# The 64-expert stage: eleven buffers for the blocks' activations, down products ten blocks behind, gates in groups of four tiles, and the first eleven blocks on ScalarE and GpSimd

## What is computed

```python
x = layernorm(hidden).reshape(-1, 128)             # T = 2048 tokens
shared = silu(x @ sg_w.T) * (x @ su_w.T) @ sd_w.T  # one expert of width 128 for all tokens
scores = sigmoid(x @ gate_w.T) + gate_bias         # T x 64
group_scores = scores.reshape(T, 8, 8).max(-1)     # keep the best 4 groups of 8 experts
masked = scores * mask_of_best_groups
topk_w, topk_i = top_k(masked, 6); topk_w /= topk_w.sum(-1) + 1e-8
comb = zeros(T, 64).at[topk_i].add(topk_w)         # the gates: 6 of 64 are not zero
h = silu(x @ eg_w[e].T) * (x @ eu_w[e].T)          # every expert e, width 64, every token
out = hidden + shared + sum_e comb[:, e] * (h @ ed_w[e].T)
```

## Time and profile before

| what | us |
|---|---|
| median of 3 runs | 1375.47 (1373.68 to 1376.39) |
| the profiled execution | 1376.14 |
| its span, from the first to the last instruction | 1374.3 |
| PE busy in the span | 1128.8 |
| DVE busy | 883.7 |
| ACT busy | 671.6 |
| POOL busy | 576.9 |

### The profile page before, as it was taken

How to read it: one execution, slowest core, us unless ns; L and a number is a source line. 1 busy time by engine, 2 the same in 40 slices (tenths; PEclk the granted TensorE clock), 3 DMA queues, 4 the chain that set the end, 5 groups by cost and what they waited for, 6 DMA issues and landing times. The chain is left out here.

```text
span 1374.3 us, 23423 instructions
## 1 busy us (share of the span) xinstructions
PE 1128.8 (82%) x7024; PEld 882.8 (64%) x7024; DVE 883.7 (64%) x2078; ACT 671.6 (49%) x1259; POOL 576.9 (42%) x585
## 2 busy tenths in 40 slices
PE   5978899979987999719994787299287599999997
PEld 3655467758874899618883455177166377878785
DVE  6758866635552778665665586367475676777775
ACT  3556566545534444345552465057244255555553
POOL 3306855610000324462332434536082266767674
PEclk9998899987998999959997897589586799999998
DMA  7999600000002300041112820122420244454443
GB/s 198 218 183 182 75 1 2 1 1 1 1 4 72 105 1 13 21 129 45 47 40 65 224 61 26 41 77 60 156 96 1 75 129 118 124 118 126 116 123 98
DMA packets 112633, 109.01 MB, mean 79 GB/s; under 512 B 16757, under 2 KB 81916, under 8 KB 112530
## 3 DMA queue, kind: packets, MB, share of 16 engines
q1 hardware_dynamic: 106562, 98.34, 31.2%
q0 software_dynamic: 4544, 8.47, 1.8%
q10 hardware_dynamic: 1424, 0.92, 0.2%
HBM read 74.44 MB, written 34.16 MB: 79 GB/s over the span
## 5 line engine op out<-in xcount | busy, mean ns | idle before, releaser
L3147 POOL TENSOR_TENSOR e_h<-e_h,e_gate 128x512 f32<-128x512 f32 x128 | 188.0, 1485 | 134.1 <-DVE e_h L3199 86.3
L3204 DVE TENSOR_TENSOR e_h_low<-e_h,e_h_high 128x512 fp32r<-128x512 f32 x132 | 117.4, 889 | 77.1 <-ACT e_h_high L3134 77.0
L3134 ACT ACTIVATE e_h_high<-e_h 128x512 fp32r<-128x512 f32 x132 | 83.5, 633 | 102.1 <-POOL e_h L3147 94.1
L2603 POOL DMA_INDIRECT sorted_y<-zT,e_zb x78 | 75.7, 970 | 129.7 <-DVE zT L2761 116.5
L3199 DVE TENSOR_TENSOR e_h<-e_s,e_ps_b 128x512 f32<-128x512 f32 x132 | 89.4, 678 | 10.5 <-ACT e_s L3119 5.7
L550 POOL DMA_INDIRECT sorted<-w_rows,w_index x64 | 70.1, 1095 | 52.8 <-DVE w_index L456 25.6
L3119 ACT ACTIVATE e_s<-e_ps_a 128x512 f32<-128x512 f32 x132 | 77.5, 587 | 25.7 <-PE e_ps_a L2195 23.9
L1784 DVE TENSOR_REDUCE u_mx<-u_ps_s 128x2 f32<-128x512 f32 (+1 forms) x96 | 64.9, 687 | 33.9 <-PE u_ps_s L1642 32.4
L1208 POOL MEMSET t_vbd<- 128x1024 f32 x1 | 1.0, 956 | 157.8 <-POOLq L1144 157.8
L1220 POOL TENSOR_TENSOR t_sm<-t_sm,t_den 128x1024 f32<-128x1024 f32 x16 | 30.4, 1901 | 81.5 <-DVE t_den L1342 81.5
L2193 PE MATMUL e_ps_y<-e_h_high,ed_low 128*128 128x512 f32 x132 | 53.5, 405 | 7.2 <-DVE e_y L3208 4.8
(11 more groups left out here) (603 smaller groups left out, 3498.3 us busy)
## 6 DMA issues: line engine op xcount, KB each, us to landing
e_gate<-gates_by_expert SPq DMA_DIRECT2D x256, 128.0 KB, 3.2
sorted<-blank SPq DMA_DIRECT2D x2, 8775.0 KB, 80.2
a_q<-q_part SPq DMA_DIRECT2D x24, 256.0 KB, 6.9
w_raw<-in_L1w SPq DMA_DIRECT2D x24, 256.0 KB, 4.5
e_zb<-sorted SPq DMA_DIRECT2D x78, 65.0 KB, 1.8
w_rows<-sorted_y SPq DMA_DIRECT2D x16, 256.0 KB, 5.0
q_part<-a_q_parts SPq DMA_DIRECT2D x8, 256.0 KB, 4.2
q_part<-w_q_parts SPq DMA_DIRECT2D x8, 256.0 KB, 5.4
```

The costliest lines, as they stand in the source:

```text
L2603: nc.gpsimd.indirect_dma_start(out=y_dram, out_offset=bass.IndirectOffsetOnAxis(ap=at, axis=0), in_=y[j % NY][:, :], in_offset=None, bound ...
L3134: nc.scalar.activation(h_parts[k % 3][0][:, :], h[k % 3][:, :], ACT.Copy).then_inc(high_ready, 1)
L3147: nc.gpsimd.tensor_tensor(h[c % 3][:, :], h[c % 3][:, :], gate[pair % SLOTS][:, :], ALU.mult)\
L3204: nc.vector.tensor_tensor(h_parts[k % 3][1][:, :], h[k % 3][:, :], h_parts[k % 3][0][:, :], ALU.subtract).then_inc(low_ready, 1)
```

## The change

`h` gets eleven buffers (`RING`): five of its own, four in the room of `zT` and two in the room of a raw weight tile. All three engines do the second half of a step for block n - 10 (`LAG`) in place of n - 1 and n - 3: ACT rounds `h_high`, DVE makes `h_low` and PE adds the down product of block n - 10, all in step n. For the first eleven blocks (`EARLY`), ACT copies `ps_b` to `h` and POOL multiplies it by `s`, so that DVE has no part in them. DVE chooses the gates by groups of four tiles: those of groups 0, 1 and 2 ahead of its steps, those of group 3 in three pieces behind steps 15, 18 and 21. PE turns them and ACT stores them in steps 3, 12, 14 and 26. The sigmoid is taken in two pieces, the masking of a group's four tiles becomes one instruction in place of four, the gates take the room of the logits, and the turned gates that of `y`.

```diff
+    RING = 11
+    LAG = RING - 1
+    EARLY = RING
+    TURN_AT = {3: 0, 12: 1, 14: 2, 26: 3}
+    CHOOSE_AT = {15: 0, 18: 1, 21: 2}
...
         @block.tensor
             def step(n, c, g):
                 if alive(n, 0):
-                    wait(pe, h_ready, n - 2)
+                    wait(pe, b_out if isinstance(n, int) and n - 3 < EARLY else h_ready, n - 2)
                     ...
-                if isinstance(n, int) and n == 2:
-                    turn_gates()
-                if alive(n, 3):
-                    k, group = of(c, g, 3)
-                    pe.wait_ge(low_ready, n - 2)
+                if isinstance(n, int) and n in TURN_AT:
+                    turn_gates(TURN_AT[n])
+                if alive(n, LAG):
+                    k, group = of(c, g, LAG)
+                    pe.wait_ge(low_ready, n - LAG + 1)
...
         @block.scalar
             def step(n, c, g):
                 ...
                     nc.scalar.activation(s[c % 3][:, :], ps_a[c % 3][:, :], ACT.Silu).then_inc(s_ready, 1)
+                if early(n):
+                    act.wait_ge(b_done, n + 1)
+                    nc.scalar.activation(h[c % RING][:, :], ps_b[c % 3][:, :], ACT.Copy).then_inc(b_out, 1)
+                if isinstance(n, int) and n in TURN_AT:
+                    store_gates(TURN_AT[n])
+                if alive(n, LAG):
+                    high(n, c, g, LAG)
...
         @block.gpsimd
+            for n in range(EARLY):
+                pool.wait_ge(s_ready, n + 1)
+                pool.wait_ge(b_out, n + 1)
+                nc.gpsimd.tensor_tensor(h[n][:, :], h[n][:, :], s[n % 3][:, :], ALU.mult).then_inc(h_ready, 1)
...
         @block.vector
+            for i in range(GROUPS - 1):
+                choose_groups(i)
+                choose_experts(i)
+                make_gates(i)
             def step(n, c, g):
-                if alive(n, 0):
+                if alive(n, 0) and not early(n):
+                    if isinstance(n, int) and n == EARLY:
+                        dve.wait_ge(h_ready, EARLY)
                     dve.wait_ge(s_ready, n + 1)
                     dve.wait_ge(b_done, n + 1)
-                    wait(dve, low_ready, n - 2)
-                    nc.vector.tensor_tensor(h[c % 3][:, :], s[c % 3][:, :], ps_b[c % 3][:, :], ALU.mult)\
+                    wait(dve, low_ready, n - RING + 1)
+                    nc.vector.tensor_tensor(h[c % RING][:, :], s[c % 3][:, :], ps_b[c % 3][:, :], ALU.mult)\
                         .then_inc(h_ready, 1)
-                if alive(n, 1):
-                    k, _ = of(c, g, 1)
-                    dve.wait_ge(high_ready, n)
+                if alive(n, LAG):
+                    k, _ = of(c, g, LAG)
+                    dve.wait_ge(high_ready, n - LAG + 1)
                     ...
+                if isinstance(n, int) and n in CHOOSE_AT:
+                    (choose_groups, choose_experts, make_gates)[CHOOSE_AT[n]](GROUPS - 1)
```

More of the change, by code:

```diff
@@ L3029, in alive, with early @@
             return not isinstance(n, int) or 0 <= n - lag < GROUPS * BLOCKS
+        def early(n):
+            return isinstance(n, int) and n < EARLY
         def ends_group(n):
@@ L3065, in _, with turn_gates @@
         def _(pe):
[L3066 to L3073, removed]
+            def turn_gates(g):
+                pe.wait_ge(gates_ready, g + 1)
+                wait(pe, gates_out, g)
+                for j in range(GROUP):
+                    last = nc.tensor.transpose(ps_g[0:E, j * P:(j + 1) * P], G[:, g * GROUP + j, :], ident)
+                last.then_inc(gates_turned, 1)
             def step(n, c, g):
                 if alive(n, 0):
-                    wait(pe, h_ready, n - 2)
+                    wait(pe, b_out if isinstance(n, int) and n - 3 < EARLY else h_ready, n - 2)
                     at = place(c)
@@ L3098, in step, with store_gates @@
                     last.then_inc(y_turned, 1)
-            rotate_blocks(pe, step, 5)
+            rotate_blocks(pe, step, LAG + 2)
         @block.scalar
         def _(act):
[L3104 to L3113, removed]
+            for tiles in (slice(0, GROUP), slice(GROUP, TILES)):
+                act_in = L[:, tiles, :].rearrange("p a b -> p (a b)")
+                nc.scalar.activation(act_in, act_in, ACT.Sigmoid).then_inc(scores_ready, 1)
+            def store_gates(g):
+                cols = slice(g * 512, (g + 1) * 512)
+                act.wait_ge(gates_turned, g + 1)
+                if g > 0:
+                    act.wait_ge(gates_stored[g - 1], 16)
+                nc.scalar.activation(turned_gates, ps_g[0:E, :], ACT.Copy).then_inc(gates_out, 1)
+                act.wait_ge(gates_out, g + 1)
+                act.dma_start(gates_dram[:, cols], turned_gates).then_inc(gates_stored[g], 16)
             def step(n, c, g):
@@ L3163, in _ @@
[L3163 to L3185, removed]
@@ new lines, in choose_experts, with make_gates @@
+            def choose_experts(i):
+                ts = slice(i * GROUP, (i + 1) * GROUP)
+                for t in range(ts.start, ts.stop):
+                    nc.vector.max(top[:, t, :], cand[:, t, :])
+                dve.drain()
+                for t in range(ts.start, ts.stop):
+                    nc.vector.match_replace(rest[:, t, :], top[:, t, :], cand[:, t, :], -SENTINEL)
+                nc.vector.reduce_sum(den[:, ts], top[:, ts, 2:8], X)
+                dve.drain()
+            def make_gates(i):
+                ts = slice(i * GROUP, (i + 1) * GROUP)
+                nc.vector.tensor_tensor(rest[:, ts, 0:E], rest[:, ts, 0:E], cand[:, ts, 0:E], ALU.not_equal)
+                nc.vector.tensor_scalar(den[:, ts], den[:, ts], 1.0e-8, None, ALU.add)
+                dve.drain()
+                nc.vector.tensor_tensor(rest[:, ts, 0:E], rest[:, ts, 0:E], cand[:, ts, 0:E], ALU.mult)
+                nc.vector.reciprocal(den[:, ts], den[:, ts])
+                dve.drain()
+                nc.vector.tensor_tensor(G[:, ts, :], rest[:, ts, 0:E],
+                                        den[:, ts].unsqueeze(2).broadcast_to([P, GROUP, E]), ALU.mult)\
+                    .then_inc(gates_ready, 1)
@@ L3212, in step @@
                     nc.vector.tensor_tensor(rows, rows, ps_g[:, :], ALU.add).then_inc(added, 1)
-            rotate_blocks(dve, step, 5)
+            rotate_blocks(dve, step, LAG + 2)
 def arrive(nc, sem, value):
```

66 lines of the change are left out of this document (36 added, 30 removed).

## The result

The changed kernel takes 1587.64 us (median of four runs, 1584.71 to 1591.19), the kernel before in the same comparison 1374.58: the ratio is 1.154, 95% interval 1.151 to 1.157. The profiled execution took 1591.19 us with a span of 1589.4, at a mean granted clock of 0.895. The forecast was 1566, with a range of 1535 to 1615: the sign, the size and the likeliest case are as forecast, and the time is 22 us over it (25 for the profiled execution).

What follows compares the result with a forecast made beforehand. PE was taken as the bound after an opening in which it stands still. From the profiled 1376.1 us, -21 opening, +203 distance, +5 turns, +1 fourth group and +1.6 end sum to +190: 1566 us, range 1535 to 1615.

Steps and rivals of the forecast that it cites:

- the likeliest case: PE waits in each step for DVE's low part: 1566 us, about 14% slower; chance 0.82, alone spanning 1540 to 1600.
- The distance: Steps of blocks 12 to 131: PE waits for low part n - 10 behind DVE's product; 3.80 us against 2.11, +203.2.
- The opening: Before block 12's products: PE's idle stretch shrinks, gates take 20.5 us, block 12 begins about 1086 against 1107.2; -21 us.
- an opening that ends after 1095, with DVE's gate operations stretched beside POOL: Sign that the forecast is wrong; it expected block 12's products near 1086.
- The turns: Steps 12, 14 and 26: ACT's rounding waits behind transposes, copies and a transfer; each step 1.7 us longer, +5 in all.
- The fourth group and the end: Group 3's gate pieces fit DVE's free time, +1 us; ten down products after the last block take 8.0, +1.6.
- The clock falls: Rival: PE's rests lower the clock in the steps, 5.55 us each; 1776 us, or 1671 if half the time; chance 0.08.
- clock 1.00 up to the end: Sign that the forecast is right: PE's granted clock stays at the higher level despite its wait in each step.
- POOL comes first: Rival: the low part waits for POOL's multiply in each step, 1.08 us more, 130 in all; 1696 us; chance 0.06.
- Faster: Rival: down products find their parts ready, a step is 2.04 us; 1349 us in all; chance 0.04.

## Why the prediction was right, and where its sizes were off

**The distance** was right in place and price: step 3.79 against 3.80, and in the step shown 1.14 to the sixth matmul (1.13 forecast), 1.77 from there to the end of the low part at 1134.64 (1.77), 0.06 to PE (0.13) and 0.80 for the down matmuls (0.77), 3.77 in all. PE waited 123 times and 192.1 us in all, where some 120 times and 200 were forecast. The two runs that take the wait away, by distance and by order, both bring the step to 2.04, so it is shown that what costs is what stands ahead of the part in two queues. The prediction named DVE's product; ACT's Silu, which it mentioned, turned out to be nearly as strong a hold.

**The opening** was mis-sized. Counted from the sigmoid's start, block 12 was to begin after 26.6 us, and it took 1097.27 - 1057.44 = 39.8: 13.2 more. The gates took 29.9 in place of 20.5 (9.4 of it): the prediction took contention as nearly free "since POOL loses as much as it wins", and DVE lost 11.3 by it. The first low part took 1.76 (1.0), its down product 1.45 in place of 0.77 at the lower clock (0.7), and step 11, at that clock too, 6.19 in place of 3.80, from 1091.08 to 1097.27 (2.4). The prediction had named this itself as a sign of being wrong: "an opening that ends after 1095, with DVE's gate operations stretched beside POOL". The Trainium skill, SBUF — State Buffer, "Who interferes with whom", has a rule for it: an instruction of VectorE with two inputs in SBUF, or a tensor_scalar in its two-port mode, shuts out GpSimd's reads or is shut out. The traces agree with the first, which went from 0.43 to 1.41; a tensor_scalar went from 0.17 to 1.26, but in which mode it ran, no run here shows.

**The turns** were right as waits, and what came with them was left out. Steps 12 to 17, 26 and 27 are 14.8 longer than 3.79 each, against 5 + 1 forecast, and 12.3 of that goes when ACT rounds first. From the sixth matmul to the down product the turns' steps 12, 14 and 26 take 4.08, 3.55 and 3.48 in place of 1.83, together 5.6 more, where 1.7 each was forecast. (Four transposes did take 0.60 at the full clock, in step 14, though half of 1.06, from which the prediction had it, is 0.53.) But about half of the 14.8 is no wait: in these eight steps the products take 14.0 us in place of 8 x 1.14, and the down products 9.0 in place of 8 x 0.80, 7.5 in all, since many of the matmuls are 0.43 apart. This is the lower clock, which the sum had at nothing once the opening was over.

**The fourth group and the end.** One step behind a piece (16) is still 1.5 longer when the turns are hidden, 1 forecast. Ten down products at the end took 1580.92 + 0.40 - (1570.63 + 0.23) = 10.5 against 8.0. The prediction expected the higher clock there; from 1570 to 1580 it was 0.83, and one low part took 1.77 beside POOL.

**The sum.** Block 12 began at 1097.27 against 1086, 11.3 over (13.2 less the 1.96 by which the stage began earlier than before); the steps of blocks 12 to 131 took 1570.63 + 0.23 - 1097.27 = 473.6 against 456 + 5 + 1 = 462, 11.6 over; the end is 2.5 over. 1566 + 25.4 = 1591.4, the profiled execution's 1591.19 but for rounding. About 12 of these 25 us are matmuls at the lower clock's distance: 2.3 around step 11, 7.5 in the eight steps, and 2.2 in steps 63 and 64. The turns, the pieces and the end together went over by some 14, where the prediction allowed 4 for them; the time stayed in the range because the 12 allowed for the step and the 17 for the opening were not used up. That they covered for the other terms was luck.

**The rivals.** *The clock falls*: not in the usual step, 1.00 from 1230 to 1240 with PE at rest for 1.44 in each; but in places it did, and the sign "clock 1.00 up to the end" did not come. In steps 63 and 64, between 1306 and 1316, the step took 5.44 and 4.54. Why it fell there stays open. *POOL comes first*: three times (low parts of 1.76 and 1.11 in the opening and 1.77 at the end), not in each step. *Faster*: had the parts been ready, the forecast said 1349 (-21 opening, -8 steps, +2 end). With two steps of distance that kernel exists, and it is 12.8 faster than before, not 27. In its stage block 13 begins 17.6 earlier; from there to block 131 it takes 248.6, as before 248.7, since the steps 13 to 28, with the pieces and turns, take 4.7 more (37.97 against 33.27), and the steps behind them, with three shorter group ends (2.39 + 2.43 each in place of 3.98 + 2.40 at the first), give that back; the end is 4.8 longer.

## What to carry to other kernels

The lag between two engines is the difference of their positions in their own lists, not the age of the data: raising every engine's lag together took the room from two steps to none, and one step on the waiting engine alone, or taking up the old block ahead of the new one, gave all of it back. When one of two queues holds a result back, undoing it shows nothing if the other holds it as long, so undo both together as well as each alone. Work moved into an idle stretch is priced beside what runs there: 18.6 us of VectorE became 29.9 beside GpSimd.

## What the runs showed of the hardware that I had not expected

With PE at rest for 1.44 of each 3.79 us, in nearly all of 120 steps, the granted clock was 1.00 in most of the stage (1230 to 1240, for one). It fell twice in the steady part, to 0.83 from 1160 to 1170, behind the last turn, and to 0.81 and 0.85 from 1300 to 1320; after the rest of 10.70 it was 0.50. An operation on four numbers per partition with a single tensor input (the `TENSOR_SCALAR` above) was drawn out from 0.17 to 1.26 beside GpSimd, as much as one on 256. POOL's own multiply, started behind a low part, took 1.62 on average in place of 1.29, and cost nothing, since nobody waited for it.
